# A perceiver layer on one core: self attention and feed forward written as one program, with the last output product taken by row tiles

## The chip, the cores and the metric

The kernel runs on one core of a Trainium2 chip. The metric is the device time of one execution in microseconds (us). A program here has five engines: TensorE (PE, matrix products and transposes), VectorE (DVE), ScalarE (ACT), GpSimd (POOL) and SyncE (SP, which issues the DMA transfers). Each works through its own list of instructions in order and waits on semaphores for the others.

## The reference

The input `x` has 8 batches of 64 rows of 2048 elements, so 512 rows, or four row tiles of 128. All is float32.

```python
x = x + _L0_xattn_ref(_layernorm(x), ctx_4096)            # softmax(q k^T) k, 1601 keys
x = x + _L0_attn_ref(_layernorm(x), w_q, w_k, w_v, w_o)   # 32 query heads, 8 key/value heads of 128, causal
h = _layernorm(x)
q = h @ Wq_w.T; scores = q @ keys.T                       # router: 16 wide, 64 experts
gate = softmax of the 16 largest scores, 0 elsewhere
z = h @ A_w.T                                             # "down", 2048 -> 512 = 64 experts x rank 8
x = x + (z * gate per expert) @ B_w.T * 2                 # "up", 512 -> 2048
```

## The kernel before, in words

Float32 products are made from two parts of each operand, a high part (`_hi`, written by ACT as a copy) and a low part (`_lo`, the remainder, written by DVE or POOL). `three_products` (L703) issues hi x hi, hi x lo and lo x hi into the same bank of PSUM.

Three stages follow each other, each in its own `Block`, whose end all engines wait for: `cross_attention`, `self_attention` (L722), `feed_forward` (L1103). `h_hi` and `h_lo` hold the normalized rows, transposed: 16 chunks of 128 inputs by 512 rows.

`self_attention` works in 9 turns over 8 groups of heads. The first is turn 0, turns 1 to 7 are a hardware loop, turn 8 (`GROUPS`) is written out. Turn g multiplies six weight tiles (`PROJ`, `project`, 48 products of 128x512 each) for group g, and in between does the attention of group g-1 (`attend_scores`, `probs_transpose`, two times `attend_values`). At its end it multiplies that attention with `w_o`, 4 column chunks by 4 row tiles (`times_w_o`), 16 outputs of 128x512, 12 products each. DVE adds each to `rows` (L993). Turn 8 has no projections: its attention and its 16 outputs stand one behind the other. There DVE also takes the statistics of each piece (`bn_stats`, L997). The outer loop of the 16 outputs is the column chunk, the inner one the row tile, so no row is complete before the last chunk.

A weight tile goes through a ring of two slots: SP loads `raw` (L833), ACT copies it to `w_hi` (L867), POOL subtracts into `w_lo` (L853). A slot of `raw` is free when POOL is done with it, a slot of `w_hi` and `w_lo` when the product that reads it is.

`feed_forward` loads and zeroes its small tensors, works out the four rows' rsqrt (`rows_rsqrt`, L657), normalizes (L677), transposes the 16 quads of h (4 transposes of 128x128 make a quad, `rows_transpose_slot` L690, three PSUM banks in turn), then the four quads of the first down tile, then the router's weights (`ff_wq`, `ff_keys`, L1416). Then come the router's 32 products (L1421, L1422), and the down products `down(a)`, a = 0 to 3. In `down(a)`, the quads of the next weight tile are transposed in between, a quad after each 12 products (`transpose_item`, L1402). The router's scores follow the first quarter of `down(0)`, the gates' transpose follows `down(0)`. `up(c)` makes the output.

## Time and profile before

| | us |
|---|---|
| median of 3 runs | 1854.04 (1852.74 to 1854.44) |
| the profiled execution, its own time | 1853.19 |
| its span, first to last instruction | 1851.3 |
| PE busy | 1718.7 (93%) |
| DVE, ACT, POOL busy | 719.5, 753.1, 856.6 |

The span is the time from the first to the last instruction. PE is busy for nearly all of it, so what is left to look for is where it is not, and where its granted clock is below full speed (the page's row of tenths). The page's busy shares of the other engines are averages over stages with different limits. An idle time in brackets at the end of a timeline row stands before that row, with the instruction that ended it.

### The profile page before, as it was taken

Reading aid. Unit: us, or ns where it says so; the run is one execution under the profiler, and the core shown is the slowest. Engines: PE = TensorE matmul, PEld = TensorE weight load, DVE = VectorE, ACT = ScalarE, POOL = GpSimd, SP = SyncE. Lnnn points to the kernel's source line nnn. Section 1 sums busy time; section 2 is a strip of 40 time slices with the busy share of each in tenths; the row PEclk is TensorE's granted clock in tenths of the full one; section 3 lists DMA queues with packets and bytes.
Section 4 is the critical chain, followed back from the end, with each engine's and each line's share of the span. In section 5 each row is a group of like instructions: output and inputs, shape, how many; then the busy total and the mean of one; then the engine's idle time right before and its main releaser. Section 6 shows DMA issues by size and latency. Waiting matters only on the chain. (4 is left out here: it accounts for less than half of the span.)

```text
span 1851.3 us, 21688 instructions
## 1 busy us (share of the span) xinstructions
PE 1718.7 (93%) x8781; PEld 1421.0 (77%) x8781; DVE 719.5 (39%) x1088; ACT 753.1 (41%) x936; POOL 856.6 (46%) x300
## 2 busy tenths in 40 slices
PE   4899999999999954999999999999999999978999
PEld 3788888888888833887887878878878888756677
DVE  3666758577685676010211202202022030135523
ACT  2677877777778842222131121222212212211321
POOL 0488777877778832334424333333342433312010
PEclk8999999999999976999999999999999999979999
DMA  9155565556555423232332233223223232211113
GB/s 318 38 193 178 184 202 176 189 190 194 175 187 191 126 80 114 73 87 91 91 91 91 83 97 91 68 94 87 91 91 91 91 91 84 98 46 49 46 69 114
DMA packets 178351, 219.20 MB, mean 118 GB/s; under 512 B 4160, under 2 KB 102464, under 8 KB 176224
## 3 DMA queue, kind: packets, MB, share of 16 engines
q1 hardware_dynamic: 178288, 218.32, 37.4%
q8 instruction: 44, 0.72, 0.2%
q14 instruction: 19, 0.16, 0.0%
HBM read 209.92 MB, written 8.39 MB: 118 GB/s over the span
## 5 line engine op out<-in xcount | busy, mean ns | idle before, releaser
L853 POOL TENSOR_TENSOR sa_w_lo<-sa_raw,sa_w_hi 128x2048 fp32r<-128x2048 f32 x80 | 367.8, 4598 | 621.0 <-ACT sa_w_hi L867 621.0
L375 POOL TENSOR_TENSOR xa_nat_lo<-xa_raw_a,xa_nat_hi 128x1024 fp32r<-128x1024 f32 (+1 forms) x112 | 267.4, 2409 | 129.5 <-ACT xa_nat_hi L389 129.5
L525 DVE TENSOR_TENSOR xa_ct_lo<-xa_ps_t,xa_ct_hi 128x833 fp32r<-128x833 f32 (+1 forms) x256 | 252.9, 988 | 185.4 <-ACT xa_ct_hi L414 102.3
L705 PE MATMUL sa_ps_mm<-h_hi,sa_w_hi 128*128 128x512 f32 x768 | 302.6, 394 | 1.4 <-DVE h_lo L928 1.4
L707 PE MATMUL sa_ps_mm<-h_hi,sa_w_lo 128*128 128x512 f32 x768 | 299.1, 389 | 0.0
L706 PE MATMUL sa_ps_mm<-h_lo,sa_w_hi 128*128 128x512 f32 x768 | 299.0, 389 | 0.0
L993 DVE TENSOR_TENSOR rows<-rows,sa_ps_mm 128x512 f32<-128x512 f32 x128 | 88.0, 687 | 493.4 <-PE sa_ps_mm L707 493.4
L414 ACT ACTIVATE xa_ct_hi<-xa_ps_t 128x833 fp32r<-128x833 f32 (+1 forms) x256 | 215.0, 840 | 152.0 <-PE xa_ps_t L575 105.1
L867 ACT ACTIVATE sa_w_hi<-sa_raw 128x2048 fp32r<-128x2048 f32 x80 | 153.0, 1913 | 286.5 <-PE sa_ps_mm L707 286.5
L375 POOL TENSOR_TENSOR xa_nat_lo<-xa_raw_b,xa_nat_hi 128x1024 fp32r<-128x1024 f32 x88 | 210.9, 2404 | 55.7 <-ACT xa_nat_hi L389 52.9
L705 PE MATMUL sa_ps_mm<-sa_w_hi,sa_o_hi 128*128 128x512 f32 x512 | 204.0, 398 | 6.9 <-ACT sa_q_t L899 4.8
L707 PE MATMUL sa_ps_mm<-sa_w_hi,sa_o_lo 128*128 128x512 f32 x512 | 203.0, 396 | 0.0
L706 PE MATMUL sa_ps_mm<-sa_w_lo,sa_o_hi 128*128 128x512 f32 x512 | 203.0, 396 | 0.0
L632 PE MATMUL xa_ps_o<-xa_nat_hi,xa_e_t 128*128 128x512 f32 (+1 forms) x416 | 186.0, 447 | 10.1 <-DVE xa_acc L506 5.1
L612 PE MATMUL xa_ps_s<-xa_ct_hi,xa_q_t 128*128 128x512 f32 (+2 forms) x512 | 143.9, 362 | 38.3 <-DVE xa_ct_lo L525 20.1
L705 PEld LDWEIGHTS sa_ps_mm<-h_hi,sa_w_hi 128*128 128x128 f32 x768 | 144.2, 188 | 35.1 <-ACT sa_q_t L899 2.3
L707 PEld LDWEIGHTS sa_ps_mm<-h_hi,sa_w_lo 128*128 128x128 f32 x768 | 144.1, 188 | 30.4
L632 PE MATMUL xa_ps_o<-xa_nat_lo,xa_e_t 128*128 128x512 f32 (+1 forms) x416 | 167.4, 402 | 0.0
L706 PEld LDWEIGHTS sa_ps_mm<-h_lo,sa_w_hi 128*128 128x128 f32 x768 | 144.3, 188 | 28.8
L612 PEld LDWEIGHTS xa_ps_s<-xa_ct_hi,xa_q_t 128*128 128x128 f32 x512 | 91.1, 190 | 66.7 <-issue 18.7
L612 PE MATMUL xa_ps_s<-xa_ct_lo,xa_q_t 128*128 128x512 f32 (+2 forms) x512 | 136.7, 348 | 0.0
L899 ACT ACTIVATE sa_q_t<-sa_ps_mm 128x512 f32<-128x512 f32 x32 | 19.2, 599 | 266.6 <-PE sa_ps_mm L707 266.6
(173 smaller groups left out, 2294.6 us busy)
## 6 DMA issues: line engine op xcount, KB each, us to landing
xa_raw_a<-in_ctx SPq DMA_DIRECT2D x32, 1536.0 KB
xa_raw_b<-in_ctx SPq DMA_DIRECT2D x32, 1536.0 KB, 7.1
sa_raw<-in_L_attn_w_q SPq DMA_DIRECT2D x32, 1024.0 KB, 6.0
sa_raw<-in_L_attn_w_o SPq DMA_DIRECT2D x32, 1024.0 KB, 5.0
sa_raw<-in_L_attn_w_k SPq DMA_DIRECT2D x8, 1024.0 KB, 5.4
sa_raw<-in_L_attn_w_v SPq DMA_DIRECT2D x8, 1024.0 KB, 5.3
xa_xq<-in_x SPq DMA_DIRECT2D x8, 512.0 KB, 5.4
xa_raw_a<-in_ctx SPq DMA_DIRECT2D x32, 128.0 KB
```

What stands on the lines that cost most here:

```text
L375: pool.tensor_tensor(nat_lo[0:p, u % NAT, :, :], src, nat_hi[0:p, u % NAT, :, :].bitcast(F32), ALU.subtract).then_inc(nat_pool, 1)
L414: i = act.activation(ct_hi[:, t % RING, 0:w], ps_t[:, t % RING, 0:w], ACT.Copy)
L525: i = dve.tensor_tensor(ct_lo[:, t % RING, 0:w], ps_t[:, t % RING, 0:w], ct_hi[:, t % RING, 0:w].bitcast(F32), ALU.subtract)
L612: i = pe.matmul(ps_s[:, lo:hi], q_t[:, g, :], ct[:, t % RING, lo:hi], start=g == 0 and ct is ct_hi, stop=g == DC - 1 and ct is ct_lo)
L632: ins = pe.matmul(group_bank(c), e_t[0:p, x, k, :], nat[0:p, u % NAT, half, :], start=first and (k, half) == tiles[0] and nat is nat_hi, s ...
L705: pe.matmul(out, hi, mov_hi, start=first, stop=False)
L706: pe.matmul(out, hi, mov_lo, start=False, stop=False)
L707: return pe.matmul(out, lo, mov_hi, start=False, stop=last)
L853: pool.tensor_tensor(w_lo[:, n, :], raw[:, n, :], w_hi[:, n, :].bitcast(F32), ALU.subtract).then_inc(w_lo_done, 1)
L867: act.activation(w_hi[:, n % 2, :], raw[:, n % 2, :], ACT.Copy).then_inc(w_hi_done, 1)
L899: act.activation(dst, ps_mm[:, n % 2, :].rearrange("p (b q) -> p b q", q=LQ), ACT.Copy).then_inc(proj_out, 1)
L993: dve.tensor_tensor(part, part, ps_mm[:, n % 2, :], ALU.add).then_inc(wo_added, 1)
```

## The change

`self_attention` and `feed_forward` become one function, `decoder`, in one `Block`. All tensors have fixed places, so that those of the feed forward share memory with those of the attention that are dead by then. PSUM is one tensor of eight banks. The parts:

1. The loop covers turns 1 to 6, and turn 7 (`LAST`) is written out. In it, the scores of group 8's attention follow the last projection. The transposes of its probabilities follow the first column chunk of turn 7's output product, the two value products come before the output of chunk 3, row tile 2, and after the last one.
2. Group 8's output product runs by row tiles: row tile outside, chunks 0, 1, 3, 2 inside. All four chunks of `w_o` therefore lie in memory at once: chunk 0 in the ring, chunk 1 in the columns of `h_hi` and `h_lo` that belonged to row tile 3, chunk 2 in the second slot of the ring (its low part by DVE), chunk 3 where the queries and probabilities were. SP loads chunks 3 and 2 into `normed` ahead of turn 7's first load.
3. During row tile 0's outputs the first down tile is transposed, a quad behind each; during those of row tile r the four quads of h for row tile r-1, two behind the second output and two behind the third. Each row tile has its own rsqrt (`row_rsqrt_steps`), and ACT normalizes one half of its columns, DVE the other. Only row tile 3's quads come behind the last output, with three quads of the second down tile.
4. The router's weights are loaded and transposed in turn 0, behind the first projection; the zeroing of `ff_wq_t` (848 columns in place of 2048) is in POOL's prologue.
5. Behind the router's products `down(0)` runs in one piece of 48 products over all 512 rows. Then come a quad and the router's scores. The transpose of the gates comes before the last quarter of `down(1)`, the expansion of the gates behind it.
6. `rows_rsqrt` makes three steps in place of four.

The diff, cut to its core:

```diff
-            self_attention(nc, x1, w_q, w_k, w_v, w_o, rows, h_hi, h_lo, row_bn, ident)
-            feed_forward(nc, a_w, b_w, wq_w, keys, rows, h_hi, h_lo, row_bn, ident, out.rearrange("b q d -> (b q) d"))
+        decoder(nc, x1, w_q, w_k, w_v, w_o, a_w, b_w, wq_w, keys, rows, row_bn, ROWS_AT + 4 * RT * D,
+                out.rearrange("b q d -> (b q) d"))
...
-    for _ in range(4):
+    for _ in range(3):
...
+ENDING_WO = [0, 1, 3, 2]
...
+            sp.wait_ge(wq_done, 1)
+            sp.dma_start(normed[:, 1, :].rearrange("p (h n) -> p h n", h=HG), chunk(3)).then_inc(fourth_in, 16)
+            sp.dma_start(normed[:, 0, :].rearrange("p (h n) -> p h n", h=HG), chunk(2)).then_inc(third_in, 16)
+            turn(LAST)
...
+            project_group(LAST)
+            attend_scores(GROUPS)
+            for c in range(NCOL):
+                for r in range(RT):
+                    if c == NCOL - 1 and r == 2:
+                        attend_values(GROUPS, 0)
+                    times_w_o(LAST, c, r)
+                if c == 0:
+                    probs_transpose(GROUPS)
+            attend_values(GROUPS, 1)
...
+            for r in range(RT):
+                for i, c in enumerate(ENDING_WO):
+                    ending_w_o(r, i, c)
+                    if r == 0:
+                        t_slot("w", 0, i)
+                    elif i in (1, 2):
+                        t_slot("h", r - 1, 2 * i - 2)
+                        t_slot("h", r - 1, 2 * i - 1)
...
+            for r in range(RT):
+                for i, c in enumerate(ENDING_WO):
+                    n = NCOL * r + i
+                    add_rows(GROUPS, n, r, c)
+                    dve.wait_ge(wo_added, 1 + WO_BEFORE + n + 1)
+                    ins = dve.bn_stats(row_bn[:, r, c, :], rows[:, r, c * 512:(c + 1) * 512])
+                    if r == 0:
+                        evacuate("w", 0, i)
+                    elif i in (1, 2):
+                        evacuate("h", r - 1, 2 * i - 2)
+                        evacuate("h", r - 1, 2 * i - 1)
+                link(ins)
+                layernorm(r)
```

On PE, at the start of turn 8, before: all of the attention in a row, between the outputs of turn 7 and those of turn 8 (`sa_ps_s` scores, `sa_ps_p` transposed probabilities, `sa_ps_o` values).

```order
L1033 MATMUL sa_ps_s<-sa_k_t,sa_q_t 128x64 x16
L1040 MATMUL sa_ps_p<-ident,sa_prob 128x128 x8
L1054 MATMUL sa_ps_o<-sa_p_t,sa_v 128x256 x8
```

Now, from the last value transpose of turn 7 to the end of the attention (`sf_ps` is all of PSUM, `...` stands for projections and output products; the last two rows are the first quads of the ending).

```order
L1448 MATMUL sf_ps<-ident,sa_v_t 128x128 x4
...
L1418 MATMUL sf_ps<-sa_k_t,sa_q_t 128x64 x16
...
L1425 MATMUL sf_ps<-ident,sa_prob 128x128 x8
...
L1439 MATMUL sf_ps<-sa_p_t,sa_v 128x256 x4
...
L1439 MATMUL sf_ps<-sa_p_t,sa_v 128x256 x4
...
L1532 MATMUL sf_ps<-ident,raw 128x128 x4
```

The four pieces are no longer neighbours: products stand between each piece and the one that needs its result.

On DVE, in the last 16 outputs, before: an addition and the statistics of a piece, and nothing else.

```order
L993 TENSOR_TENSOR rows<-rows,sa_ps_mm 128x512
L997 BN_STATS row_bn<-rows 128x6
L993 TENSOR_TENSOR rows<-rows,sa_ps_mm 128x512
L997 BN_STATS row_bn<-rows 128x6
L993 TENSOR_TENSOR rows<-rows,sa_ps_mm 128x512
L997 BN_STATS row_bn<-rows 128x6
```

Now, the last two outputs of row tile 1 and its layernorm (the rows L182 to L188 are its rsqrt, ten small operations).

```order
L1253 TENSOR_TENSOR rows<-rows,sf_ps 128x512
L1325 BN_STATS row_bn<-rows 128x6
L1291 TENSOR_TENSOR h_lo<-sf_ps,h_hi 128x4x128 x2
L1253 TENSOR_TENSOR rows<-rows,sf_ps 128x512
L1325 BN_STATS row_bn<-rows 128x6
L674 BN_AGGR mv<-row_bn 128x2
L182 TENSOR_SCALAR rs_w<-mv 128x1
...
L188 TENSOR_SCALAR rs_w<-rs_w 128x1
L1302 TENSOR_SCALAR shift<-mv,rs_w 128x1
L1306 TENSOR_SCALAR normed<-rows,mv,rs_w 128x1024
```

DVE now has the quads' low parts and a layernorm between the additions.

## Rows read from the trace of the kernel before

**Rows 1.** The page, busy tenths of 40 slices of 46.3 us: PE and its granted clock.
```profile
PE   4899999999999954999999999999999999978999
PEclk8999999999999976999999999999999999979999
```

**Rows 2.** PE's waits, 1600 to 1740 us: total us, times, longest.
```profile
PE ff_ps_t L690 <- DVE ff_normed L677: 9.2, 1, 9.2
PE sa_ps_p L1040 <- DVE sa_prob L981: 8.0, 1, 8.0
```

**Rows 3.** Timeline of PE around turns 7 and 8: start us, us, what.
```profile
1585.24 0.50 PE L705 MATMUL sa_ps_mm<-sa_w_hi,sa_o_hi 128*128 128x512 f32 x1 [0.69 <-ACT sa_q_t L899]
...
1630.15 3.68 PE L1033 MATMUL sa_ps_s<-sa_k_t,sa_q_t 128*128 128x64 f32 x32
...
1653.21 0.77 PE L705 MATMUL sa_ps_mm<-sa_w_hi,sa_o_hi 128*128 128x512 f32 x1 [2.09 <-DVE sa_o_lo L986]
...
1656.28 0.40 PE L706 MATMUL sa_ps_mm<-sa_w_lo,sa_o_hi 128*128 128x512 f32 x1
```

**Rows 4.** Timeline of PE in a turn of the loop: the attention's three pieces.
```profile
918.43 3.68 PE L1033 MATMUL sa_ps_s<-sa_k_t,sa_q_t 128*128 128x64 f32 x32
932.93 1.03 PE L1040 MATMUL sa_ps_p<-ident,sa_prob 128*128 128x128 f32 x8
944.81 1.14 PE L1054 MATMUL sa_ps_o<-sa_p_t,sa_v 64*128 64x256 f32 x8
```

**Rows 5.** Timeline of DVE, turn 8: first and last of 16 additions, last statistics.
```profile
1657.64 0.69 DVE L993 TENSOR_TENSOR rows<-rows,sa_ps_mm 128x512 f32<-128x512 f32 x1 [4.58 <-PE sa_ps_mm L707]
...
1699.64 0.69 DVE L993 TENSOR_TENSOR rows<-rows,sa_ps_mm 128x512 f32<-128x512 f32 x1 [1.39 <-PE sa_ps_mm L707]
1700.36 0.69 DVE L997 BATCH_NORM_STATS2 row_bn<-rows 128x6 f32<-128x512 f32 x1
```

**Rows 6.** Timeline of PE, last output product to the router's first.
```profile
1699.20 0.40 PE L707 MATMUL sa_ps_mm<-sa_w_hi,sa_o_lo 128*128 128x512 f32 x1
...
1725.84 1.16 PE L1416 MATMUL ff_ps_t<-ident,ff_wq 16*128 16x16 f32 x16 [0.16 <-DVE ff_w_lo L1312]
...
1728.25 0.79 PE L1421 MATMUL ff_ps_r<-h_hi,ff_wq_t 128*128 128x512 f32 x1 [1.10 <-DVE ff_wq_t L1334]
```

**Rows 7.** Timeline of DVE, the layernorm of one row tile in self attention's prologue.
```profile
715.09 0.25 DVE L660 BATCH_NORM_AGGREGATE sa_mv<-row_bn 128x2 f32<-128x24 f32 x1
715.38 0.15 DVE L663 TENSOR_SCALAR sa_rs_w<-sa_mv 128x1 f32<-128x1 f32 x1
...
716.52 4.34 DVE L671 SCALAR_TENSOR_TENSOR sa_rs_w<-sa_rs_w 128x1 f32<-128x1 f32 x1
...
722.65 1.34 DVE L677 TENSOR_SCALAR sa_normed<-rows,sa_mv,sa_rs_w 128x2048 f32<-128x2048 f32 x1
```

**Rows 8.** Timeline of POOL at the same time: a weight tile's low part.
```profile
716.33 4.52 POOL L853 TENSOR_TENSOR sa_w_lo<-sa_raw,sa_w_hi 128x2048 fp32r<-128x2048 f32 x1 [6.22 <-ACT sa_w_hi L867]
```

**Rows 9.** Timeline of ACT: the exponential over 1024 columns, and a quad of h.
```profile
1637.96 1.06 ACT L880 ACTIVATE sa_prob<-sa_s 128x1024 f32<-128x1024 f32 x1 [5.70 <-DVE sa_s L976]
...
1710.76 0.60 ACT L1253 ACTIVATE h_hi<-ff_ps_t 128x512 fp32r<-128x512 f32 x1 [0.26 <-PE ff_ps_t L690]
```

**Rows 10.** Timeline of DVE: the low part of the same quad.
```profile
1711.39 0.69 DVE L1299 TENSOR_TENSOR h_lo<-ff_ps_t,h_hi 128x512 fp32r<-128x512 f32 x1 [0.16 <-ACT h_hi L1253]
```

**Rows 11.** Timeline of PE: a quad of a weight tile between products of `up`.
```profile
1800.31 0.39 PE L707 MATMUL ff_ps_mm<-ff_w_hi,ff_z_lo 128*128 128x512 f32 x1
1800.54 0.60 PE L1402 MATMUL ff_ps_t<-ident,ff_raw 128*128 128x128 f32 x4
1800.90 0.48 PE L705 MATMUL ff_ps_mm<-ff_w_hi,ff_z_hi 128*128 128x512 f32 x1
```

**Rows 12.** Timeline of DVE: the first and the last operation of the gates' chain.
```profile
1741.18 0.42 DVE L1342 COPY ff_scores<-ff_ps_r 128x256 f32<-128x256 f32 x1 [2.47 <-PE ff_ps_r L1429]
...
1748.74 0.42 DVE L1367 TENSOR_TENSOR ff_gate<-ff_chosen,ff_g_inv 128x256 f32<-128x256 f32 x1
```

**Rows 13.** The page, DMA issues: KB each, median us to landing.
```profile
sa_raw<-in_L_attn_w_o SPq DMA_DIRECT2D x32, 1024.0 KB, 5.0
```

More of the change, by code:

```diff
@@ L716, with transpose_order @@
 UNIT_SM = 2 * RT * 2
-def self_attention(nc, x1, w_q, w_k, w_v, w_o, rows, h_hi, h_lo, row_bn, ident):
+ENDING_WO = [0, 1, 3, 2]
+EXPERTS, RANK, RD, TOP = 64, 8, 16, 16
+NZ = EXPERTS * RANK
+ZC = NZ // P
+SCALING = 2.0
+ITEMS = ZC + NCOL
+WQ_LO, WQ_W = 32, 48
+KIB = 1024
+def transpose_order():
+    order = [("w", 0, q) for q in range(4)]
+    order += [("h", r, q) for r in range(RT) for q in range(QUADS)]
+    order += [("w", m, q) for m in range(1, ITEMS) for q in range(4)]
+    return order
@@ new lines, in decoder, with after @@
+        prob = at("sa_prob", [P, UNIT_SM, LQ], 140 * KIB)
+        k_t = at("sa_k_t", [P, ROWS], 144 * KIB)
+        v_t = at("sa_v_t", [P, ROWS], 146 * KIB)
+        v = at("sa_v", [P, RT, HD], 148 * KIB)
+        p_t = at("sa_p_t", [P, 2 * RT, P], 150 * KIB)
+        o_hi = at("o_hi", [P, HG, ROWS], 154 * KIB, F32R)
+        o_lo = at("o_lo", [P, HG, ROWS], 162 * KIB, F32R)
+        small = [170 * KIB]
+        def after(name, shape, dt=F32):
+            size = 4
+            for n in shape[1:]:
+                size *= n
+            t = at(name, shape, small[0], dt)
+            small[0] += (size + 31) // 32 * 32
+            return t
@@ L915, in _ @@
+            evacuate("w", 2, 2)
+            for a in range(ZC):
+                act.wait_ge(gx_done, a + 1)
+                act.activation(gates[:, a, :], ps_r[:, a % 2, :], ACT.Copy).then_inc(gx_out, 1)
+            z_high(0)
+            evacuate("w", 2, 3)
+            z_high(1)
+            for m in range(3, ITEMS):
+                for q in range(4):
+                    evacuate("w", m, q)
+                if m - 1 < ZC:
+                    z_high(m - 1)
         @block.vector
@@ L955, in _, with softmax_shift @@
             dve.wait_ge(mask_ready, 3)
-            def turn(g):
-                n_proj, n_wo = kind(g)
-                if not n_wo:
-                    dve.memset(s_inv[:], 0.0).then_inc(wo_added, 1)
-                    return
-                last = isinstance(g, int) and g == GROUPS
+            def softmax_shift(g):
                 here = base + SOFTMAX_LINKS * (g - 1)
-                def step(ins, n):
-                    ins.then_inc(chain, 1)
-                    dve.wait_ge(chain, here + n)
@@ L999, in _, with heads_low, add_rows @@
-            turns(dve, turn)
+            def heads_low(g, half):
+                for b2 in range(2):
+                    dve.wait_ge(o_hi_done, 4 * (g - 1) + 2 * half + b2 + 1)
+                    dve.tensor_tensor(o_rows(o_lo, half, b2), o_ps(b2), o_rows(o_hi, half, b2).bitcast(F32),
+                                      ALU.subtract).then_inc(o_lo_done, 1)
+            def add_rows(g, n, r, c):
+                dve.wait_ge(wo_bank, NCOL * RT * (g - 1) + n + 1)
+                part = rows[:, r, c * 512:(c + 1) * 512]
+                dve.tensor_tensor(part, part, ps_mm[:, n % 2, :], ALU.add).then_inc(wo_added, 1)
@@ new lines, in _ @@
+            link(i)
+            for r in range(RT):
+                i = dve.match_replace(out=rest[:, 1, r, :], in_to_replace=best[:, r, 8:16], in_values=rest[:, 0, r, :],
+                                      imm_value=-3.0e38)
+            link(i)
+            link(dve.tensor_tensor(chosen[:], rest[:, 1, :, :], sc[:], ALU.not_equal))
+            dve.wait_ge(exp_done, 1)
+            link(dve.tensor_tensor(chosen[:], chosen[:], expo[:], ALU.mult))
+            link(dve.tensor_reduce(g_sum[:], chosen[:], AX.X, ALU.add))
@@ L1001, in _ @@
+            for c in range(NCOL):
+                for r in range(RT):
+                    n = RT * c + r
+                    dve.wait_ge(o_done, n + 1)
+                    part = rows[:, r, c * 512:(c + 1) * 512]
+                    dve.tensor_tensor(part, part, ps_mm[:, n % 2, :], ALU.add).then_inc(o_added, 1)
+                    if ZC + c + 1 < ITEMS:
+                        evacuate("w", ZC + c + 1, r)
         @block.tensor
@@ L1423, in _ @@
[L1423 to L1431 removed]
+                i = down_part(0, c, slice(0, ROWS))
+            i.then_inc(z_done, 1)
+            t_slot("w", 1, 3)
```

848 lines of the change are left out of this document (451 added, 397 removed).

## The prediction

> **What bounds the kernel now.** I read the page's slices first: PE is at nine tenths or more nearly everywhere, with a dip in slices 35 and 36 to 37 (about 1620 to 1712 us) besides the one between cross attention and self attention near 650 to 740 us, and the granted clock falls in the same places [rows 1]. The waits of PE then name the two longest pauses of the late part: 8.0 us for the softmaxed probabilities and 9.2 us for the normalized rows [rows 2]. Elsewhere PE runs product after product, so the change can gain only in these pauses, in the slow clock behind them, or by giving PE less to do. It hardly does the last: the same products are issued.
>
> The timeline gives the two gaps their whole size. Gap A: turn 7's outputs end where the scores begin, at 1630.15, and turn 8's first output product starts at 1653.21 [rows 3], 23.06 us. Gap B: the last output product starts at 1699.20 and so hands over at about 1699.43, and the router's first product starts at 1728.25 [rows 6], 28.8 us. Between them lie 16 outputs, one each 2.80 us ((1699.64 - 1657.64) / 15) [rows 5]. Behind each gap PE runs at the lower of its two clock levels for a while: the first output's first seven products take 1656.28 - 1653.21 = 3.07 us, against 7 x 0.233 = 1.63 at the full clock (0.233 is 2.80 / 12), so 1.4 us more [rows 3, 5].
>
> **The change part by part.**
>
> *Gap A, the attention of group 8 between products.* Its own PE work at full clock is 3.68 + 1.03 + 2 x 1.14 = 7.0 us [rows 4]; there the same pieces are woven between products, with no wait. For that cover to hold here each chain must be shorter than what stands before the next piece. DVE's softmax starts at the scores' end, 1630.15 + 3.68, and lasted as long as PE's wait of 8.0 us [rows 2, 3], ACT's 1.06 included [rows 9]. Now it has four outputs, 11.2 us, as cover, less up to 1.4 us for the two additions that are queued in it. The probabilities' copy to the value products has 30 us. The value products' parts go through ACT and DVE under two or more outputs, the second half under the first output's start only, and that one is needed by row tiles 2 and 3, 20 us later. So gap A becomes 7.0 us: 23.1 - 7.0 = 16.1 saved. With no idle PE in front, the slow first products go too: 1.4. Sum for A: 17.5. If the cover failed altogether nothing would be saved here; bounds 0 and 17.5, and I take 17.5, as the woven turns of the loop show no wait.
>
> *Do the weights arrive?* Turn 8's four chunks need, in POOL's order: turn 7's third tile, chunk 3, turn 7's fourth, chunk 0, chunk 1, 4.5 us each [rows 8]. I lay them out from the start of turn 7's outputs (0), where chunk c's outputs end at 11.2 (c+1), plus about 1 to 2 us for the woven pieces. ACT may fill a slot when its reader is done: 11.2, 22.4, 34. POOL is then busy 13 to 18, 18 to 22 (chunk 3), 24 to 29, 37 to 42 (chunk 0), 42 to 47 (chunk 1). Turn 8's outputs start at 44.8 + 1.1 + 2.3 = 48, and chunk 1 is wanted 3.2 us later: a margin of 4 us. The first down tile is loaded after chunk 0, at 42, lands 5.0 us later [rows 13] at 47, and is wanted at 51. Chunk 2's low part is on DVE, behind ACT's copy (2 x 1.06 [rows 9] from about 48 + 1.2): four times 0.69 [rows 5], at most 2.8 us, so it ends at 48 + 6. The first addition waits behind it, and the third output behind that addition: it wants to start at 48 + 6.5. Cost 0 to 1, taken as 0.2. The two 1 MB loads that SP issues ahead of turn 7's first one delay it by up to 10 us at 5.0 us each [rows 13]; ACT wants the tile some 15 us after its issue, so 0.
>
> *The 16 outputs by row tile.* The products are the same; 16 quads are new between them. A quad costs from 1800.54 to 1800.90, 0.36, and the next product is 0.09 longer (0.48 against 0.39) [rows 11]: 0.43 with rounding. 16 x 0.43 = 6.9 us added. PE's row tile is then 4 x 2.80 + 4 x 0.43 = 12.9 us. DVE's: 4 additions and 4 statistics, 8 x 0.72 = 5.7 [rows 5]; 4 low parts of 0.69 [rows 10] = 2.8; a layernorm: aggregate 0.29, ten steps of 0.19 ((716.52 - 715.38) / 6), the shift 0.19, half a normalization 0.67 (1.34 / 2) [rows 7], in all 3.1. That is 11.6 of 12.9. ACT's is 4 x 0.60 + 1.06 [rows 9]. The layernorm of row tile r-1 stands in front of the first addition of row tile r: it ends 1.4 + 3.1 = 4.5 us after the last output, the addition at 5.2, and PE needs it at 5.6; ACT's half ends 4.9 after, and the quad wants it at 5.6. I get no wait, by 0.4 to 0.7 us.
>
> *Gap B, what is left of it.* After the last output PE waits for: addition and statistics to 1.6, the layernorm to its shift 2.4 (sum 4.0), ACT's half 1.06 (5.1). Then four quads of h, at the pace of the slow clock 0.60 + 0.26 = 0.86 each [rows 9], and the last one's ACT and DVE parts, 0.3 + 0.60 + 0.69 behind it: 5.2 + 3.4 + 1.6 = 10.2, and with three quads of the next weight tile among it, I put the router's start at 11.2 (bounds: 10.2, and 13 if these quads come in front of all). So B goes from 28.8 to 11.2: 17.6 saved, minus the 6.9 and the 0.2 from above = 10.5. The router's start is on the slow clock before and after (0.79 for its first product [rows 6]), no change.
>
> *Feed forward.* Three of the four quads of the second down tile leave `down(0)`: 3 x 0.43 = 1.3 saved. The gates' chain from scores to gate takes 1749.16 - 1741.18 = 8.0 us with two low parts of a weight tile (1.4) and a wait in it [rows 12]; those low parts now come behind it. Its cover is three quarters of `down(1)`, 3 x 2.80 + 2 x 0.43 = 9.3 us. It fits by at least 1.3 us; if it did not, PE would wait for the rest.
>
> *Router's weights in turn 0.* 16 transposes of 1.16 us and one more go onto PE, which is full there: +1.3 [rows 6]. Their loads and copies lie beside the first projections. Bounds 0.8 (full clock) and 1.5.
>
> *Self attention's prologue.* Three operations fewer in each of two rsqrts, 2 x 0.59; both are on the way to the first projection. Against that POOL zeroes 848 columns while the first of them runs. The trace shows what that does: DVE's small operation took 4.34 us where its neighbours take 0.15, and it ended when POOL's 4.52 us did [rows 7, 8]. So up to 0.8 us may be given back. Net -0.8, bounds -1.2 and 0.
>
> The Trainium skill ("SBUF — State Buffer", Who interferes with whom) calls this an exclusive lock: DVE and GpSimd share a pair of ports, and an operation of DVE with both inputs in SBUF, or in a two-port mode, waits for all of a running GpSimd operation. By that rule the trace agrees (4.34 us), and the rule speaks against the change at one place: chunk 2's low part on DVE reads SBUF alone, and would start late by what POOL still has of chunk 1. By my layout POOL is done 4 us earlier, so rule and sum give the same; if POOL were late by its whole tile, it would add up to 4.5 us, which is in the range.
>
> Sum: -17.5 - 10.5 - 1.3 + 1.3 - 0.8 = -28.8. From the span 1851.3: 1822.5. The profiled execution's own time is 1.9 above its span (1853.19), and the median of the runs 0.85 above that; -28.8 on 1854.04 is 1825.2, which I give as 1825.
>
> **The rivals.**
>
> *R1, the ending is paced by DVE.* DVE has 11.6 of 12.9 us per row tile, and its order is fixed: an addition that waits behind a low part, which waits for ACT, holds PE's next output. For it: the margins above are 0.4 to 0.7 us, and a weight that is late by 4 us is enough as well. Against it: three banks for quads, and nothing in my layout is late. Price: 1 to 3 us in each of four row tiles, 4 to 12 us: 1829 to 1837.
>
> *R2, lockstep, slower than before.* If each of the 16 quads held PE until its ACT and DVE parts were through (0.26 + 0.60 + 0.69 + hand-overs, 2.0 in place of 0.43, 1.6 x 16 = 25) and each of three layernorms stood bare in front of the next row tile (3.1 + 1.06 = 4.2, 13 in all), the ending would give back 38 us and the time would be 1863. It decides when DVE lags PE by more than one output, 2.8 us, in every row tile. Against it: 11.6 is under 12.9, and the parts of a quad have a whole output as cover.
>
> *R3, gap A only moves.* If the softmax or the values found no cover (POOL holding DVE's operations for 4.5 us each at the softmax's two full-SBUF steps), 8 to 9 us come back: 1834. Against it: POOL has no tile in that stretch but the one that ends within 3 us of the scores' end.
>
> *R4, nothing much happens,* because other waits close in at each place; it would need 25 us of new waits with no row for them.
>
> **How the numbers follow.** Forecast 0.77, R1 0.11, R3 0.05, R2 0.04, R4 0.01, and 0.02 for something better than I see (router start earlier, prologue's full 1.2). The forecast's own spread: B's left-over +-1.5, prologue and turn 0 +-0.6, the start of the ending 0 to +4.5, thus 1822 to 1831. The range for 8 in 10 takes some of R1 and leaves 3 us for steps that overlap better: 1819 to 1833. A difference of 0.2% (3.7 us) is about what a measurement of this kernel tells from no change; faster by more than that: the forecast, R1, R3 and the better case, 0.95; same 0.01; slower 0.04.
>
> **What would show each step.** In the changed profile: PE's wait for the probabilities is gone and the scores stand right behind the last projection; from the last product of turn 7 to the first of turn 8 about 1.1 us. The 16 outputs with their quads take about 51.7 us. From the last output product to the router's first about 11 us, with one idle stretch of about 5. `down(0)` is 48 products without a break. A wait of PE for DVE's additions inside the ending would speak for R1, one for low parts at every quad for R2. The forecast is wrong if the ending takes over 55 us, or if the time lies above 1833.

## The result, and the profile after

| | before | after |
|---|---|---|
| median of the runs (us) | 1854.2 (1852.7 to 1855.1, 4 runs) | 1813.4 (1810.6 to 1813.9, 4 runs) |
| the profiled execution: span, own time | 1851.3, 1853.2 | 1811.7, 1813.5 |

The ratio is 0.978, 95% interval 0.976 to 0.979: 40.8 us less, where 28.8 were forecast. A second series of five runs of the same kernel (E14 below) gave 1816.2 (1813.5 to 1818.4), 0.980 (0.978 to 0.981), 37.8 us less. Both medians lie below the predicted range, 1819 to 1833: something was missed. Each series of the experiments below stands beside its own series of the kernel before, on one of five chips; the medians of those go from 1853.4 to 1854.7. One of the six executions of experiment E5 took 4358.7 us, more than twice the others, for a cause that stays open, and is left out of E5's numbers.

The page of the changed kernel, its slices of 45.3 us, which answer to [rows 1]. The second dip of PE is gone but for one slice, and in the row of the granted clock only the fall between cross attention and self attention is left. A slice hides a short one: over 1680 to 1700 us, where the last layernorm stands bare, the granted clock was 0.83. Such a stretch at the lower level is called a dip below.
```profile
PE   4899999999999973999999999999999999999899
PEclk9999999999999985999999999999999999999999
```
PE's waits from 1560 us to the end, which answer to [rows 2]. The 8.0 us for the probabilities are gone; of the 9.2 us for normalized rows 5.8 are left:
```profile
PE sf_ps L1532 <- ACT normed L1151: 7.1, 4, 5.8
PE sf_ps L708 <- DVE ff_z L1314: 2.0, 1, 2.0
PE sf_ps L1418 <- ACT sa_q_t L1086: 0.7, 1, 0.7
```
PE's timeline at the places of [rows 3] and [rows 6]: the scores of group 8 ahead of turn 7's outputs, its values behind them, the first output product of turn 8, the last one, and the way to the router's first product (x3 of the scores, because the view ends there; they are 32):
```profile
1578.68 0.55 PE L1418 MATMUL sf_ps<-sa_k_t,sa_q_t 128*128 128x64 f32 x3 [0.69 <-ACT sa_q_t L1086]
...
1628.23 1.14 PE L1439 MATMUL sf_ps<-sa_p_t,sa_v 64*128 64x256 f32 x8
1629.30 0.50 PE L708 MATMUL sf_ps<-w_hi,o_hi 128*128 128x512 f32 x1
...
1681.96 0.39 PE L710 MATMUL sf_ps<-w_hi,o_lo 128*128 128x512 f32 x1
1688.19 3.65 PE L1532 MATMUL sf_ps<-ident,normed 128*128 128x128 f32 x16 [5.84 <-ACT normed L1151]
1691.63 2.28 PE L1532 MATMUL sf_ps<-ident,raw 128*128 128x128 f32 x12
1693.66 0.47 PE L1582 MATMUL sf_ps<-h_hi,ff_wq_t 128*128 128x512 f32 x1
```
The same landmarks in both traces give the account of the two profiled executions, in us, after minus before for each stretch:

| stretch | forecast | measured |
|---|---|---|
| to the end of turn 7's projections (1585.24, now 1578.68) | +0.5 | -6.56 |
| to the first output product of turn 8 (1653.21, now 1629.30) | -16.1 | -17.35 |
| to the last one (1699.20, now 1681.96) | -1.4 + 6.9 + 0.2 = +5.7 | +6.67 |
| to the router's first product (1728.25, now 1693.66) | -17.6 | -17.35 |
| to the end (1851.3, now 1811.7) | -1.3 | -5.01 |
| sum | -28.8 | -39.60 |

The three stretches that the change was argued on came out within 1.3 us each. What was missed lies in stretches where the order of PE's work hardly changes. There the products of one line stand closer. Of a turn's 16 outputs, the first product and three from the middle, from PE's timeline of the kernel before, and then the same of the changed kernel, with the scores behind them:
```profile
873.52 0.50 PE L705 MATMUL sa_ps_mm<-sa_w_hi,sa_o_hi 128*128 128x512 f32 x1 [0.69 <-ACT sa_q_t L899]
...
896.03 0.40 PE L705 MATMUL sa_ps_mm<-sa_w_hi,sa_o_hi 128*128 128x512 f32 x1
896.26 0.40 PE L706 MATMUL sa_ps_mm<-sa_w_lo,sa_o_hi 128*128 128x512 f32 x1
896.50 0.40 PE L707 MATMUL sa_ps_mm<-sa_w_hi,sa_o_lo 128*128 128x512 f32 x1
```
```profile
874.28 0.50 PE L708 MATMUL sf_ps<-w_hi,o_hi 128*128 128x512 f32 x1 [0.69 <-ACT sa_q_t L1086]
...
896.17 0.39 PE L708 MATMUL sf_ps<-w_hi,o_hi 128*128 128x512 f32 x1
896.40 0.39 PE L709 MATMUL sf_ps<-w_lo,o_hi 128*128 128x512 f32 x1
896.63 0.39 PE L710 MATMUL sf_ps<-w_hi,o_lo 128*128 128x512 f32 x1
...
917.93 0.44 PE L1418 MATMUL sf_ps<-sa_k_t,sa_q_t 128*128 128x64 f32 x3
```
From the first product to the scores (32 again, of which the view has 3) it is 918.43 - 873.52 = 44.91 us before ([rows 4] for the scores) and 917.93 - 874.28 = 43.65 after: 1.26 us a turn. The mean distance of two products in the middle is 0.2334 us before and 0.2267 after. The projections' products stood at 0.2267 in both kernels; the output products took on their pace.

### The profile page after: what moved, and what is told of

It reads as the page before. It is cut to its first block, busy times and chain, and to the rows that moved or that the text cites. A ratio compares the mean times of both kernels' runs of the same rounds, so it can differ in the third digit from the quotient of the medians.

```text
span 1811.7 us, 21596 instructions
## 1 busy us (share of the span) xinstructions
PE 1700.0 (94%) x8781; PEld 1414.6 (78%) x8781; DVE 721.4 (40%) x1111; ACT 756.9 (42%) x940; POOL 851.1 (47%) x299
## 4 chain that ended last, share of the span: by engine, by line
PE 58%; DVE 2%; ACT 1%; issue 0%
PE sf_ps L708 18%; PE sf_ps L710 17%; PE sf_ps L709 17%; PE sf_ps L1418 2%; PE sf_ps L1532 1%; PE sf_ps L1439 1%; PE sf_ps L693 0%; DVE normed L680 0%; PE sf_ps L1425 0%; DVE h_lo L1192 0%; DVE rs_w L668 0%; ACT normed L1151 0%; ACT sa_q_t L1086 0%; PE sf_ps L1582 0%; PE sf_ps L1583 0%
## 5 line engine op out<-in xcount | busy, mean ns | idle before, releaser
L1007 POOL TENSOR_TENSOR w_lo<-raw,w_hi 128x2048 fp32r<-128x2048 f32 x77 | 354.1, 4599 | 567.7 <-ACT w_hi L1056 567.7
L708 PE MATMUL sf_ps<-h_hi,w_hi 128*128 128x512 f32 x800 | 316.2, 395 | 1.6 <-DVE h_lo L1192 1.6
L710 PE MATMUL sf_ps<-h_hi,w_lo 128*128 128x512 f32 x800 | 311.8, 390 | 0.0
L709 PE MATMUL sf_ps<-h_lo,w_hi 128*128 128x512 f32 x800 | 311.5, 389 | 0.0
L708 PE MATMUL sf_ps<-w_hi,o_hi 128*128 128x512 f32 x528 | 208.0, 394 | 6.1 <-ACT sa_q_t L1086 4.1
L710 PE MATMUL sf_ps<-w_hi,o_lo 128*128 128x512 f32 x528 | 205.7, 390 | 0.0
L709 PE MATMUL sf_ps<-w_lo,o_hi 128*128 128x512 f32 x528 | 205.6, 389 | 0.0
L708 PEld LDWEIGHTS sf_ps<-h_hi,w_hi 128*128 128x128 f32 x800 | 150.2, 188 | 36.4 <-ACT sa_v_t L1086 2.0
L710 PEld LDWEIGHTS sf_ps<-h_hi,w_lo 128*128 128x128 f32 x800 | 150.1, 188 | 32.0
L709 PEld LDWEIGHTS sf_ps<-h_lo,w_hi 128*128 128x128 f32 x800 | 150.3, 188 | 29.9
```

Source lines behind the costliest of these rows:

```text
L708: pe.matmul(out, hi, mov_hi, start=first, stop=False)
L709: pe.matmul(out, hi, mov_lo, start=False, stop=False)
L710: return pe.matmul(out, lo, mov_hi, start=False, stop=last)
L1007: pool.tensor_tensor(w_lo[:, n, :], raw[:, n, :], w_hi[:, n, :].bitcast(F32), ALU.subtract).then_inc(w_lo_done, 1)
```

## The experiments

**What the theories are.** A product here takes a stationary operand of 128x128, a part of the attention's output o (in `up` a part of z), and a moving one of 128x512, a part of a weight. Theory P: the pace hangs on where in SBUF the stationary operand starts. Before, `o_hi` and `o_lo` stood behind six small tiles (32, 64, 256 and three times 64 bytes, 544 in all) in the same stack as the weights, and so started 32 bytes past a multiple of 512; the changed kernel gives each tile an address by hand, and they start at a multiple of 512. The rival, theory S: the merge itself does it (one PSUM tensor, the peeled turn, other neighbours). Beside them stand the prediction's own terms.

**E1, o moved by 96 bytes in the kernel before.**
```diff
+        pad = sb("sa_pad", [P, 24])
         o_hi = sb("sa_o_hi", [P, HG, ROWS], F32R)
```


> The kernel before, with o_hi and o_lo alone 96 bytes further on, from 32 bytes past a multiple of 128 to a multiple of 128. Theory P (the start of the stationary operand sets the pace of its products): the output products of all eight groups go from 0.2334 to 0.2267 us, 1.26 us a turn, so 10.1 us less, about 1844 us; the 16 output products between two turns' boundaries take 43.7 us in place of 44.9. Theory S (the pace came from the merge itself: one PSUM tensor, the turn's code, or the neighbours in the turn): no change, 1854 us, within 1 us, and 44.9 us a turn.

Measured: 1852.6 us against 1854.7, ratio 0.999 (0.998 to 1.000), 44.72 us for a turn's outputs and 0.2324 us a product. That was a miss: neither the whole gain nor nothing. A multiple of 128 bytes is not what counts.

**E2 and E3, o moved by 32 or 64 bytes in the changed kernel.**
```diff
-        o_hi = at("o_hi", [P, HG, ROWS], 154 * KIB, F32R)
-        o_lo = at("o_lo", [P, HG, ROWS], 162 * KIB, F32R)
+        o_hi = at("o_hi", [P, HG, ROWS], 154 * KIB + 32, F32R)
+        o_lo = at("o_lo", [P, HG, ROWS], 162 * KIB + 32, F32R)
```


> The changed kernel, with o_hi and o_lo (and z_hi, z_lo, which lie there too) 32 bytes further on, off their multiple of 128. Theory P: a turn's 16 output products take 44.9 us again, up's products slow too (0.2329 against 0.2296), together 10 to 11 us more, about 1824 us, which is the predicted time. Theory S: no change, 1813 us.

> The changed kernel, with o_hi and o_lo 64 bytes further on: a multiple of 64, not of 128. Theory P with a unit of 64 bytes: 1813 us and 43.7 us a turn. Theory P with a unit of 128 bytes: as with 32 bytes, about 1824 us and 44.9 us a turn. Theory S: 1813 us.

Measured: 1826.5 us (1825.3 to 1829.2) with 32 bytes, ratio to before 0.986 (0.984 to 0.987), and 1824.5 in the one run with 64. The changed kernel loses 10 to 13 us by nothing but the 32 bytes, and 8 to 11 with 64, by its one run. From E2's profile, the first output product of that turn and the scores behind the 16:
```profile
876.13 0.50 PE L708 MATMUL sf_ps<-w_hi,o_hi 128*128 128x512 f32 x1 [0.69 <-ACT sa_q_t L1086]
...
921.03 3.68 PE L1418 MATMUL sf_ps<-sa_k_t,sa_q_t 128*128 128x64 f32 x32
```
That is 44.90 us, against 44.91 before the change, and E3 has the same. Theory S falls: the merge is all there, and the pace is the old one.

**E4 and E6, series of products with chosen starts, behind the changed kernel's last output.**
```diff
+            for n, (so, mo) in enumerate(probes):
+                for k in range(48):
+                    s0 = (k % 3) * P + so // 4
+                    m0 = (k % 3) * 512 + mo // 4
+                    pe.matmul(ps_r[:, n % 3, :], z_hi[:, k % 4, s0:s0 + P], w_lo[:, 0, m0:m0 + 512],
+                              start=k == 0, stop=k == 47)
```


> The changed kernel, with 15 further series of products behind its last output, whose results nobody reads (the 36 or 32 products of a series lie back to back, 128 x 512 each): ten series of 36 whose stationary and moving operands start at (0,0), (32,0), (64,0), (96,0), (128,0), (16,0), (0,32), (0,64), (32,32), (8,0) bytes past a multiple of 512, then five of 32 products, two to each stationary operand, that start at 0, 64, 128, 192, 256 bytes. Theory P: the series at 0 and 128 take 0.2267 us a product, those at 32, 16 and 8 take 0.2334; 64 and 96 tell whether the unit is 64 or 128 bytes, and the moving operand's start does nothing or is a second cause. Theory S: all series alike. Time 1813 us and some 120 us for the series.

> The changed kernel, with 20 series of 48 products behind its last output, whose results nobody reads. Starts of the stationary and moving operand, in bytes past a multiple of 512: (0,0), (256,0), (192,0), (224,0), (160,0), (48,0), (320,0), (384,0), (448,0), (480,0), (0,128), (0,256), (0,384), (0,448), (64,64), (128,128), (64,32), (160,128), (384,128), (256,256). Theory P2, modulo 512 and by the difference of the starts alone: the four series with equal starts take 0.2267 us a product, (64,32) and (160,128) as (32,0) did, 0.2333, and (384,128) as (256,0); (0,128) as (384,0). A theory by the stationary start alone puts (64,64), (128,128) and (256,256) beside (64,0), (128,0) and (256,0): 0.2337, 0.2326 and what (256,0) shows. No series is below 0.2267 if that is the floor of a product.

Measured, from the starts of the products in each series (the first 8 or 12 of one left out), us a product. Each of the two kernels ran once:

| start of stationary, of moving (bytes past a multiple of 512) | us |
|---|---|
| (0,0) (256,0) (0,256) (64,64) (128,128) (256,256) (32,32) (384,128) (16,0) | 0.2267 to 0.2269 |
| (192,0) (448,0) (0,64) | 0.2289 to 0.2292 |
| (8,0) | 0.2307 |
| (128,0) (384,0) | 0.2325, 0.2326 |
| (32,0) (48,0) (64,0) (96,0) (160,0) (224,0) (320,0) (480,0) (0,32) (0,128) (0,384) (0,448) (64,32) (160,128) | 0.2330 to 0.2344 |

34 neighbouring products of three series, from E6's timeline of PE: (256,0), (160,0) and (64,64). The last of the 34 has 0.39 us itself, so their distances are (7.87 - 0.39) / 33 = 0.2267 us and (8.09 - 0.39) / 33 = 0.2333.
```profile
1819.95 7.87 PE L1663 MATMUL sf_ps<-w_lo,o_hi 128*128 128x512 f32 x34
...
1853.10 8.09 PE L1663 MATMUL sf_ps<-w_lo,o_hi 128*128 128x512 f32 x34
...
1964.44 7.87 PE L1663 MATMUL sf_ps<-w_lo,o_hi 128*128 128x512 f32 x34
```
So it is the two operands' starts against each other that count, not either alone: starts that are equal modulo 256 bytes give 0.2267 in the series of all eight such pairs, wherever both lie. Theory P as first put (a multiple of 64 or 128 bytes of the stationary) falls, and so does the 512 of theory P2, as the expectations of E5 and E6 call the relation of the two starts: (256,0) and (0,256) are as fast as (0,0). It explains E1: 128 against 0 is 0.2325, and E1 had 0.2324. The two groups with 0.2290 and 0.2325, and (16,0), are seen and not explained. Two products to each stationary operand (E4's last five series) gave the same order: 0.2266 at 0, 0.2334 at 64, 0.2325 at 128, 0.2289 at 192, 0.2267 at 256.

The Trainium skill ("SBUF — State Buffer", Operand start alignment) lets an fp32 operand start at any multiple of 4 bytes, and says that this is about legality, not speed. All the kernels here keep that rule, and their products still differ by 3%.

**E5, o and z at equal starts in the kernel before.**
```diff
+        pad = sb("sa_pad", [P, 120])
         o_hi = sb("sa_o_hi", [P, HG, ROWS], F32R)
...
+        pad = sb("ff_pad", [P, 72])
         z_hi = sb("ff_z_hi", [P, ZC, ROWS], F32R)
```

> The kernel before, with o_hi, o_lo 480 bytes and z_hi, z_lo 288 bytes further on, so that they start at a multiple of 512, as the weights that move against them do. Theory P2 (what sets the pace is where the stationary operand starts against where the moving one does, modulo 512 bytes; equal starts give 0.2267 us a product): a turn's 16 output products take 43.7 us in place of 44.9, eight times, and up's go from 0.2329 to 0.2296; together 10.1 + 0.6 less, about 1844 us. Theory S (the placement helps only inside the merged kernel, with its single PSUM tensor and its peeled last turn): 1852 to 1854 us, as with the move of 96 bytes.

Measured: 1843.1 us (1842.6 to 1844.3, five executions) against 1854.6, ratio 0.994 (0.993 to 0.996), 11.5 us less for 10.7 expected. The turn's outputs, from E5's profile, take 917.55 - 873.89 = 43.66 us:
```profile
873.89 0.50 PE L705 MATMUL sa_ps_mm<-sa_w_hi,sa_o_hi 128*128 128x512 f32 x1 [0.69 <-ACT sa_q_t L900]
...
917.55 3.68 PE L1034 MATMUL sa_ps_s<-sa_k_t,sa_q_t 128*128 128x64 f32 x32
```
Two pads in the old kernel give over a quarter of the whole gain.

**E15, o at 256 bytes past a multiple of 512 in the changed kernel.** The edit is E2's with 256.

> The changed kernel, with o_hi, o_lo (and z_hi, z_lo) 256 bytes further on: equal to the weights' start modulo 256 bytes, not modulo 512. If the unit is 256 bytes, as the series (256,0) and (384,128) had it, nothing changes: 43.7 us for a turn's 16 output products, 1813 to 1816 us. If it is 512 in the kernel's own order of products: 44.9 us and about 1826 us, as e2.

Measured: 1815.0 us (1811.9 to 1819.0), ratio to before 0.979 (0.977 to 0.980), and 919.26 - 875.61 = 43.65 us for the outputs. Modulo 256 holds in the kernel's own order of products.

**E7, the last turn's attention woven into turn 7, in the kernel before.** The last turn is peeled on each engine; on PE:
```diff
+                if seven:
+                    attend_scores(GROUPS)
                 if n_wo:
                     for c in range(NCOL):
                         times_w_o(g, c)
+                        if seven and c == 0:
+                            probs_transpose(GROUPS)
+                if seven:
+                    attend_values(GROUPS, 1)
```
(and `attend_values(GROUPS, 0)` ahead of the last two outputs).

> The kernel before, with the last turn's attention alone woven into turn 7 as the changed kernel has it: its scores ahead of turn 7's output products, its transposed probabilities behind the first chunk, its values in the last chunk and behind it. Everything else as before. The prediction's term A: the wait for prob and the waits behind it go and the scores run at full clock, 16.1 + 1.4 = 17.5 us less, about 1836.8 us; the ending's first output product starts at 1637 us in place of 1653. Rival: the clock's dip or the wait moves to another place and under 12 us come back, 1842 us or more.

Measured: 1840.7 us (1837.4 to 1844.4) against 1854.6, ratio 0.993 (0.991 to 0.994): 13.9 us less, not 17.5. Its timeline of PE at the ending's start shows where the other 3.5 are:
```profile
1637.21 1.14 PE L1081 MATMUL sa_ps_o<-sa_p_t,sa_v 64*128 64x256 f32 x8
1640.44 0.57 PE L705 MATMUL sa_ps_mm<-sa_w_hi,sa_o_hi 128*128 128x512 f32 x1 [2.09 <-DVE sa_o_lo L999]
...
1641.66 0.63 PE L705 MATMUL sa_ps_mm<-sa_w_hi,sa_o_hi 128*128 128x512 f32 x1
```
Outputs by column chunk want all four row tiles of o at once, so PE still waits 2.1 us for the second half's low part, and three products take 1.22 us where 0.70 is usual: the slow clock came too, 1.4 us (granted 0.91 from 1640 to 1660 us). In the changed kernel the first two row tiles need the first half only. The weaving and the row tiles share that part of the prediction's term A.

**E13, E7 and E5 together.**

> The kernel before, with the last turn's attention woven into turn 7 (e7) and o and z at a multiple of 512 bytes (e5). If the two are separate terms, they add up: e7 gained 13.9 us, e5 11.1 us, so 25 us less than before, 1829 to 1830 us, and the ending by row tiles and the feed forward's rest have to bring the other 16 us of the 40.8. If part of the faster products hides in the gap's waits: 1831 us or more.

Measured: 1828.0 us (1826.8 to 1828.7) against 1854.0, ratio 0.986 (0.984 to 0.987): 25.9 us less, where 11.5 + 13.9 = 25.4 would be the sum. The terms add up, with some luck: E13's profile has the same wait of 2.1 us ahead of the ending, but neither E7's dip there (granted 1.00 from 1630 to 1650 us) nor the one at the router. Of the changed kernel's 37.8 to 40.8 us, 12 to 15 are left for the row tiles, the feed forward and the prologue.

**E10, the normalization of all row tiles behind the changed kernel's last output.**
```diff
-                    elif i in (1, 2):
-                        t_slot("h", r - 1, 2 * i - 2)
-                        t_slot("h", r - 1, 2 * i - 1)
...
-            for q in range(QUADS):
-                t_slot("h", RT - 1, q)
+            for r in range(RT):
+                for q in range(QUADS):
+                    t_slot("h", r, q)
```


> The changed kernel, with the layernorms and the h quads of all four row tiles behind the last output product, row tile after row tile through the one buffer of normalized rows; the 16 outputs themselves in the same order. The ending loses 12 quads and its three waits (6.7 us less, some 46 us), and behind it come four times layernorm, ACT's half and four quads, 4.2 + 1.2 + 2.9 = 8.3 us each, and the three quads of a weight, about 35 us in place of 11.5. Net 16 to 17 us more, about 1830 us: what the prediction's term B rests on. Rival: DVE's additions had slowed the ending, so that more than 6.7 us come back there; the outputs would then take under 2.72 us each and the whole under 1828 us.

Measured: 1834.5 us (1832.9 to 1835.8), ratio to before 0.990 (0.989 to 0.992): 18 to 21 us more than the changed kernel, for 16 to 17 expected. PE's one wait in that stretch:
```profile
PE sf_ps L1530 <- ACT normed L1151: 22.7, 4, 5.8
```
Four layernorms stand bare, 5.7 us each, and the granted clock was 0.59 between 1680 and 1700 us. The 16 outputs take 45.4 us in place of 52.7, and from the last one to the router's first product it is 39.1 in place of 11.5, net 20 us more. So the row tiles hide three of four layernorms, as the prediction's term B had it; the estimate left the clock out.

**E11, products into two waits of the kernel before.**
```diff
+            for k in range(32):
+                pe.matmul(ps_r[:, 0, :], h_lo[:, k % DC, 0:P], h_hi[:, k % DC, :], start=k == 0, stop=k == 31)
             for n in range(NORM_T):
```
(and 6 such ahead of `up`).

> The kernel before, with products whose result nobody reads in two of PE's waits: 32 in the 9.2 us wait for the normalized rows, 6 in the 2.0 us wait ahead of up. If PE's slow stretches behind those waits follow from its idleness, the router's first products and up's first ones run at full clock: 1.4 + 1.5 us, and the quads of the normalization up to 1 us, 2.9 to 3.9 us less, about 1851 us; this is the part of the feed forward's gain that the prediction did not have. If the granted clock follows something else, 1854.5 us.

Measured: 1851.4 us (1849.9 to 1853.9) against 1853.4, ratio 0.999 (0.998 to 1.000): 2.0 us less. The first products of `up` now ran at full clock (granted 1.00 from 1792 to 1812 us). The router's did not:
```profile
1727.83 0.50 PE L1423 MATMUL ff_ps_r<-h_hi,ff_wq_t 128*128 128x512 f32 x1 [1.10 <-DVE ff_wq_t L1334]
...
1729.14 0.63 PE L1423 MATMUL ff_ps_r<-h_hi,ff_wq_t 128*128 128x512 f32 x1
1729.57 0.63 PE L1424 MATMUL ff_ps_r<-h_lo,ff_wq_t 128*128 128x512 f32 x1
```
What lay ahead of them was no longer one long wait but 18 us of transposes with short ones. Half of the theory stands: filling `up`'s wait keeps its clock; the router's dip came all the same. One profile does not settle the router's: those of E5 and E13 have no dip there, with the long wait as it was.

**E8 and E12, the last layernorm's wait filled, in the changed kernel.** The core of the edit on PE; banks, ACT's order and the semaphores follow it, and E12 has 6 more products ahead of `up`.
```diff
+            t_slot("w", 1, 0)
+            t_slot("w", 1, 1)
+            for k in range(16):
+                pe.matmul(ps_r[:, 0, :], o_lo[:, k % HG, 0:P], o_hi[:, k % HG, :], start=k == 0, stop=k == 15)
             for q in range(QUADS):
                 t_slot("h", RT - 1, q)
-            for q in range(3):
-                t_slot("w", 1, q)
+            t_slot("w", 1, 2)
```


> The changed kernel, with two of the three quads of down's second item moved from behind the last row tile's quads into the wait for its layernorm (their banks 6 and 7 are free), and 16 products behind them in the same wait whose result nobody reads. The router's products start 2 quads sooner, 1.1 to 1.7 us, and if the clock stays at its upper level through the wait, the 16 transposes of the last row tile are paced by their evacuations, 2.9 in place of 3.65 us: together 1.9 to 2.5 us less, 1811 us. If the clock falls all the same: 1812 us. If the filling reaches past the layernorm's end: no gain, 1813 to 1814 us.

> As e8 (two quads and 16 products whose result nobody reads in the wait for the last layernorm), with 6 more such products ahead of up. e8's profiled run started the router 4.8 us sooner than the changed kernel, but lost 1.4 us of it to the lower clock behind the wait ahead of up, and its other runs were up to 8 us longer. If that wait is what made them longer, all runs now lie at 1808 to 1810 us; if the spread has another cause it stays, with a median of 1814 to 1816 us.

Measured: 1815.6 (1810.4 to 1818.1) and 1815.2 (1808.8 to 1816.2), against the 1816.2 of the changed kernel's own second series: no gain that the medians can tell. In E8's profile the router's first product stands at 1688.84 in place of 1693.66, but 3.4 us of these 4.8 it had when self attention began; 1.4 are the stretch's own, and there was a dip at `up`, which the changed kernel's profile lacks (granted 0.91 from 1740 to 1760 us). The filled wait kept its clock in both profiles, granted 1.00 from 1680 to 1700 us where it had been 0.83, and E12's stretch is 1.4 us shorter as well. E12's filling ahead of `up` did not narrow the spread (1808.8 to 1816.2 us), so that wait is not its main cause.

**E9, cross attention's rings padded to 896 columns, in the changed kernel.**
```diff
-        ct_hi = sb("xa_ct_hi", [P, RING, WIDE[0]], F32R)
-        ct_lo = sb("xa_ct_lo", [P, RING, WIDE[0]], F32R)
+        ct_hi = sb("xa_ct_hi", [P, RING, 896], F32R)
+        ct_lo = sb("xa_ct_lo", [P, RING, 896], F32R)
```

> The changed kernel, with the two rings of transposed context in cross attention padded from 834 to 896 columns a slot, by which the stationary queries and probabilities and what moves against them all start at equal places modulo 256 bytes (before: 64 against 0, 8, 32 and 40 in the scores, 64 against 0 in the value products). Some 1185 products of 512 columns in cross attention. Theory P2 at full: 1185 x 0.0067 = up to 8 us less, 1805.5 us. Against it: those products come in runs of 2 to 4 between transposes, and in the other stages the first 8 to 10 products behind transposes take 0.233 us whatever their place; by that nothing changes, 1813.4 us.

Measured: 1816.2 us (1810.6 to 1817.5), no gain. In runs of four value products the distances are 0.321, 0.231 and 0.232 us with the pad and 0.324, 0.233 and 0.232 without. Behind transposes the pace is slow anyway, and runs of 2 to 4 products never reach the fast one. This profile also shows a dip that the first one of the changed kernel lacks, behind group 8's scores with only a 0.69 us wait ahead of them:
```profile
1577.45 4.71 PE L1418 MATMUL sf_ps<-sa_k_t,sa_q_t 128*128 128x64 f32 x32 [0.69 <-ACT sa_q_t L1086]
1581.92 0.77 PE L708 MATMUL sf_ps<-w_hi,o_hi 128*128 128x512 f32 x1
1582.49 0.63 PE L709 MATMUL sf_ps<-w_lo,o_hi 128*128 128x512 f32 x1
```
The scores took 4.71 us where 3.68 is usual [rows 4], and 10 products followed at 0.43 us. From the scores to turn 8's first output product it is 3.2 us longer than in the changed kernel, in E9's profile and in E15's.

**E14, the changed kernel again.**

> The changed kernel again, unaltered, as the reference for e8, e9 and e12 and for the spread of its times. If its four runs (1810.6 to 1813.9) had the whole spread, the median is 1813 us and none is above 1815. If the dips of the clock that e9's profile showed come by chance in any kernel of this form, some runs lie at 1815 to 1818 and the median is 1813 to 1816.

Measured: 1816.2 us, 1813.5 to 1818.4. Over both series the nine runs go from 1810.6 to 1818.4, with a median of 1813.9. A difference of under 4 us between versions of this kernel is not told by five runs, so no version here is shown to beat the changed one.

## Why the prediction was wrong

**The step that failed** is "It hardly does the last: the same products are issued." They are the same products, but those whose stationary operand is a part of o or z (1536 and 192) stand closer in long runs: 1.26 us in each of seven turns, and by E2's profile against the changed kernel's another 0.4 in the ending and 0.7 in `up`, 9.9 us in all. The two profiles differ by 10.8 us more than was forecast. E5 has the placement at 11.5 us by itself, in the kernel before, and E2 takes 10 to 13 us away again. With the old placement the changed kernel took 1826.5 and 1824.5 us, where 1825 was forecast for it. That it comes so near is partly luck: in E2's profile the ending (53.2 for 51.7) and turn 0 (2.9 us longer for 1.3) cost more than the forecast had, and the feed forward (4.2 us shorter for 1.3) less. The addresses stood in the diff (every tile got its own). And the trace before had 2.80 us for 12 output products [rows 5], 0.233 each, beside projections at 0.227 in the same turn; that difference asked for a cause, and the 0.233 was used as a constant.

**Gap A** (17.5 forecast): the stretch is 17.4 shorter, 16.1 of it the gap and 1.3 turn 7's faster products, and the slow first products went as well. The mechanism was right, and of the weights that were to arrive in time PE's list of waits has none. E7 adds that 2.1 us of it hang on the row tiles, which the prediction had in a clause ("needed by row tiles 2 and 3, 20 us later") and not as a condition of the term; the other 1.4 that E7 lacks is a dip that E13, with the same order, does not have.

**The ending** (forecast 51.7 us for its outputs with quads): from 1629.30 to 1682.18 (the last product's start and 0.22) 52.9. With the old placement it was 53.2 and 53.3 (E2, E3), so the faster products gave 0.4 back here and not the 192 x 0.0067 = 1.3 of a run without breaks: the runs between quads are of 12 products, and the first 6 to 10 of them stand at about 0.23 in either case. Two sizes were off. DVE's ten steps of a layernorm take 1646.61 - 1644.19 = 2.42 us in place of 1.9, since the last six, which take factors row by row from a tile, stand 0.28 apart, and [rows 7] has no small operation of that form; and ACT's half takes 1.24 in place of 1.06; these rows answer to [rows 7] and [rows 9], DVE's first:
```profile
1643.90 0.25 DVE L674 BATCH_NORM_AGGREGATE mv<-row_bn 128x2 f32<-128x24 f32 x1
1644.19 0.15 DVE L182 TENSOR_SCALAR rs_w<-mv 128x1 f32<-128x1 f32 x1
...
1644.94 0.27 DVE L187 TENSOR_SCALAR rs_w<-rs_w 128x1 f32<-128x1 f32 x1
...
1646.06 0.27 DVE L187 TENSOR_SCALAR rs_w<-rs_w 128x1 f32<-128x1 f32 x1
1646.37 0.21 DVE L188 TENSOR_SCALAR rs_w<-rs_w 128x1 f32<-128x1 f32 x1
1646.61 0.21 DVE L1302 TENSOR_SCALAR shift<-mv,rs_w 128x1 f32<-128x1 f32 x1
```
```profile
1646.86 1.24 ACT L1151 ACTIVATE normed<-rows,shift,rs_w 128x1024 f32<-128x1024 f32 x1 [3.86 <-DVE shift L1302]
```
That used up the margin of 0.4 to 0.7 us and left PE a wait of 0.41 or 0.42 us in each of three row tiles, 7.1 - 5.8 = 1.3 in all. No wait for an addition shows, so R1's mechanism, DVE's additions holding PE, did not come as it was put; DVE's layernorm held PE for 1.3 us where R1 had 4 to 12. R2 and R3 did not come.

**Gap B** (11.2 left): 1693.66 - 1682.18 = 11.5.

**Feed forward** (1.3 forecast, 5.0 measured): the three quads are 1.3. The router's and `up`'s first products ran at full clock, where before they were slow, 1.4 and about 1.5 us; the faster products of `up` make 0.6 to 0.7 of the last 0.8. How much of the 1.4 and 1.5 belongs to the change is not shown. At the router, four of the six profiles of forms of the kernel before have the dip (E5 and E13 lack it), and none of the eleven of the changed one. At `up`, the changed kernel's profile has none, but those of E3, E8, E9 and E15 do, of the eleven; of the kernel before all five without the filling have it, and E11 shows that it goes with its wait.

**Prologue and turn 0**: the first projection starts 0.77 us sooner, for 0.8 forecast. But among kernels that are the same up to there it starts anywhere from 728.8 to 732.6 us, so this agreement is luck. Most of that spread is there when cross attention ends. The last product of cross attention and the first projection, from the timelines of before and after:
```profile
682.45 0.63 PE L632 MATMUL xa_ps_o<-xa_nat_lo,xa_e_t 128*128 128x512 f32 x1
...
732.95 0.50 PE L705 MATMUL sa_ps_mm<-h_hi,sa_w_hi 128*128 128x512 f32 x1 [1.42 <-DVE h_lo L928]
```
```profile
683.18 0.40 PE L629 MATMUL xa_ps_o<-xa_nat_lo,xa_e_t 128*128 128x512 f32 x1
...
732.18 0.50 PE L708 MATMUL sf_ps<-h_hi,w_hi 128*128 128x512 f32 x1 [1.55 <-DVE h_lo L1192]
```
So the prologue itself takes 49.00 us in place of 50.50, 1.5 less, which is outside the bounds of 0 to 1.2; in all other profiles it is 49.0 to 49.5 and 50.5 to 50.7. From the first projection to the first scores it is 68.24 in place of 66.76, 1.5 us longer, for 1.3 forecast. That stretch comes in two sizes: 68.2 to 68.3 us in five profiles of the changed kernel's forms, where the granted clock was 0.74 to 0.83 from 720 to 740 us, and 69.7 to 70.3 in the other six, where it was 0.60 to 0.66.

## What to carry to other kernels

Before taking a product's duration as a constant, compare its pace between lines of one kernel that do the same work. Where it differs, look at the addresses: give the stationary and the moving operand of long runs of products starts that are equal modulo 256 bytes (runs of 12 between transposes gained little here), and mind that a small tile ahead of them in a stack shifts all that follows. And when a change rewrites the allocation, every operand's address is part of the change.

## What the runs showed of the hardware

- Back-to-back products of 128 x 512 in fp32 stood 0.2267 us apart where both operands started at the same place modulo 256 bytes and up to 0.2344 where not, with one exception: (16,0) had 0.2267 as well. The first 6 to 10 behind transposes stood at about 0.23 in either case, so by E2 against the changed kernel 192 products in runs of 12 gained 0.4 us in the ending and 0.7 in `up`, and 192 in one run 1.26. Why is open.
- The granted clock can fall with PE hardly waiting: behind 32 products of 64 columns (E9, also E15), and behind a stretch of transposes (E11). Whether it does differs between executions of one form of kernel, at 1.4 to 3.2 us each. Turn 0's two sizes are another 2.0 us, and the start of self attention moved by up to 3.8 us. Together they are enough for a spread of 8 us in kernels whose medians one would like to compare within 2.
- A wait of PE that was filled with products kept the upper clock level in all three profiles with a filling (E8, E12 and E11's two waits), where without it the granted clock fell (0.83 over 20 us at the last layernorm).
